# Cross attention on one core: keys split ahead, two copies side by side, scores in two half-width passes

## The chip, the cores and the metric

The kernel runs on one core of a Trainium2 chip. The metric is the device time of one execution in microseconds, as the median of several runs. Before the change it is 922.41 us (three runs, 921.37 to 923.53).

## The reference, cut to what matters

A two-layer transformer block on 16 rows of 128 tokens with 256 features. Layer 0 is a convolution-like mixer with a feed-forward part (8 shared units, 8 routed experts). Layer 1 is causal attention of the normed activations (queries) over a context (keys and values are both `ctx_2048`), with 16 heads of 16 features, then a routed feed-forward part (34 units). The change touches the attention of layer 1 only:

```
x = x + tanh(g) * attention(layernorm(x), ctx, ctx)        # per layer; here layer 1
scores = einsum('bhqd,bhkd->bhqk', q, k) * HEAD_DIM**-0.5   # 16 heads of 16 features
scores = where(causal, -inf, scores)
out    = einsum('bhqk,bhkd->bhqd', softmax(scores), v)
```

All products have to be close to float32. TensorE is used with operands rounded to a shorter form (fp32r); a float32 number is split in a high part (rounded) and a low part (the rest), and products of parts are added.

## The kernel before, in words

The kernel has four stages, which follow one another on every engine: the mixer (`ctx`), the feed-forward part of layer 0 (`f0`, 64 steps K), the attention (`att`) and the feed-forward part of layer 1 (`f1`, 136 steps). Every engine has its own program, written out by hand, with semaphores between them.

The attention works on 64 quads n: block b = n // 4 is one row of 128 tokens, t = n % 4 picks four heads. One quad goes through these steps:

- `scores` (TensorE, L1458 to L1463): a bf16 pass of 512 columns puts the causal mask in a bank, then two fp32r passes of 512 columns add the products. The weights are `q_split_t` (128 rows: for each of the four heads 16 features of the high part and 16 of the low part, 64 high rows and 64 low rows); the moving tiles are `k_blocks_hi` and `k_blocks_lo`, in which each head's keys stand in their own 128 columns and the rest is zero.
- `maxima` and `shifted` (VectorE, L1642, L1648): the row maximum over each head's 128 columns, and the scores less the maximum, written to `y`.
- `turned` (TensorE, L1470): four f32 transposes into another bank.
- `probs` (ScalarE, L1611): exp of that bank to `activated`.
- `values` (TensorE, L1481): four products with `v_slot`, which stand as eight instructions in the trace.

The program of TensorE (`c_tensor`, L1558) takes, in iteration n, `turned(n)`, `scores(n + 2)`, `values(n)`, and behind them whatever else falls due. At t = 2 that is `out_rows` (L1490: four transposes that bring the result of the block before to rows), at t = 3 `query_turned(b + 2)` (L1374: four transposes of the split queries of block b + 2). Then comes `turned(n + 1)`.

The program of ScalarE (`c_scalar`, L1606) takes in iteration n: at t = 0 `out_copy` (L1504, the result's bank to SBUF), then `probs(n)`, then at t = 0 `query_copy` (L1382, the turned queries to SBUF), then `key_hi(n + 4)` (L1343, which rounds the loaded keys to the high part), at t = 2 `query_normed` (L1354), at t = 3 `query_hi` (L1361). GpSimd makes the low parts (`key_lo`, L1347; `query_lo`, L1366) and two small layer norm steps (L140, L153). SyncE issues the loads of keys (256 KB a quad, six slots, L1332) and of values (L1337).

At the end of `f0` some of this is done ahead: in the last 16 of its 64 steps SyncE loads the first six key tiles, ScalarE splits the first four, TensorE turns the queries of blocks 0 and 1 (L1374, eight and five steps before the end), and in step 63 TensorE makes the scores of quads 0 and 1 before its last product.

In `f0` a step is 12 fp32r passes of 512 columns (L666), ScalarE's silu (L446), VectorE's product (L541, L546), the split of `y` in ScalarE and VectorE (L465, L311), and 6 passes of 512 columns (L702). TensorE has one step's L666 ahead of each L702.

Of the kernel before, what the change touches and what calls it, by code (L numbers as in the profile page):

```python
# [61 lines left out]
def build(nc, x, ctx_win, k_blk, v_rows, g_x, g_f, kpad, d_skip, wu0, rw0, eb0, wu1, rw1, br1,  # L62
          ident_c, anti_c, identb_c, causal_c, out):
    top = ExitStack()
    with top:
# [24 lines left out]
        gates1 = nc.dram_tensor("gates1", (E1, T), F32, kind="Internal").ap()  # L90
        x_mid = nc.dram_tensor("x_mid", (T, D), F32, kind="Internal").ap()
# [76 lines left out]
        def feed_forward(tag, E, U, gated, wu, gates, tgcol, route, final):  # L168
# [219 lines left out]
            def sync(sp):  # L388
# [16 lines left out]
                for K in range(NK):  # L405
                    Nu = K // 2
                    if K % 2 == 0 and Nu + S < 2 * U:
                        weights(sp, Nu + S)
                    for m in range(NBLK):
                        if GATES_STORE[m] == K:  # L410
                            store_gates(m)
                    if gated and K == 0:
                        for q in range(NB - 2, NB):
                            ctx.store_mixed(q)
                    if gated and K == 2:
                        for g in range(NB // BPB):
                            ctx.load_in_order(g)
                    gate_rows(K)
                    if not final and K == NK - 16:
                        attention_loads(sp)  # L420
# [7 lines left out]
            def gpsimd(pool):  # L428
                if not gated:
                    for Nu in range(2, 4):  # L430
                        w_lo(pool, Nu)
                    for K in range(FIRST):
                        y_lo(pool, K)
                deviations(pool, tag, 1)
                if not final:
                    deviations(pool, "c", 0)
                    shifts(pool, "c", 0)
                    attention_ahead_pool(pool)

            def scalar(act):  # L440
# [49 lines left out]
                for K in range(NK):  # L490
# [34 lines left out]
                    if not final:  # L525
                        attention_ahead_act(act, NK - K)
# [774 lines left out]
        KLR, KR, SR, DR, PR = 6, 4, 3, 3, 3  # L1301
# [3 lines left out]
        KM = sb("k_blocks_sb", [P, KLR, 4 * P])  # L1305
        K1 = sb("k_blocks_hi", [P, KR, 4 * P], F32R)
        K2 = sb("k_blocks_lo", [P, KR, 4 * P], F32R)
        V = sb("v_slot", [P, 2, NH1, 32])
        xc = sb("xn_c", [P, 2, D])
        xs = sb("xn_split", [P, 2, 4, 2, 64], F32R)  # L1310
        Q1 = sb("q_split_t", [P, 2, 4, P], F32R)
        mem.out_scaled = sb("out_scaled", [P, 2, 2, BLK])
        s_sh = shift_sems["c"][1]
        s_kl = ctx.s_cq + ctx.s_cg[0:2]
        s_vl = [ctx.s_cg[2], ctx.s_kt[0]]
        LOADED = 16
        s_cc = sem("c_causal_loaded")
        s_k1 = sem("c_k_hi_ready")
        s_k2 = sem("c_k_lo_ready")
        s_n = sem("c_normed")  # L1320
# [17 lines left out]

        def key_hi(act, n):
            act.wait_ge(s_kl[n % KLR], LOADED + 16 * (n // KLR + 1))  # L1340
            if n >= KR:
                act.wait_ge(s_s, n - KR + 1)
            act.activation(K1[:, n % KR, :], KM[:, n % KLR, :], ACT.Copy).then_inc(s_k1, 1)  # L1343

        def key_lo(pool, n):
            pool.wait_ge(s_k1, n + 1)
            pool.tensor_tensor(K2[:, n % KR, :], KM[:, n % KLR, :], K1[:, n % KR, :].bitcast(F32),  # L1347
                               ALU.subtract).then_inc(s_k2, 1)
# [7 lines left out]

        def query_hi(act, b):
            act.wait_ge(s_n, b + 1)
            if b >= 2:
                act.wait_ge(s_xt, b - 1)  # L1360
            act.activation(xs[:, b % 2, :, 0, :], xc[:, b % 2, :].rearrange("p (q f) -> p q f", q=4),  # L1361
                           ACT.Copy).then_inc(s_hi, 1)

        def query_lo(pool, b):
            pool.wait_ge(s_hi, b + 1)
            pool.tensor_tensor(xs[:, b % 2, :, 1, :], xc[:, b % 2, :].rearrange("p (q f) -> p q f", q=4),  # L1366
                               xs[:, b % 2, :, 0, :].bitcast(F32), ALU.subtract).then_inc(s_lo, 1)

        def query_turned(pe, b):
            pe.wait_ge(s_lo, b + 1)  # L1370
            if b > 0:
                pe.wait_ge(s_qt, b)
# [5 lines left out]
        def query_copy(act, b):  # L1378
            act.wait_ge(s_xt, b + 1)
            if b >= 2:  # L1380
                act.wait_ge(s_s, 4 * (b - 1))
            act.activation(Q1[:, b % 2].rearrange("p t q -> p (t q)"), x_bank, ACT.Copy, scale=SCALE1).then_inc(s_qt, 1)  # L1382

        def attention_loads(sp):
            for n in range(KLR):
                load_keys(sp, n)
            sp.dma_start(causal[:], causal_c).then_inc(s_cc, 16)
            sp.dma_start(identb[:], identb_c).then_inc(s_cc, 16)
            load_values(sp, 0)
            load_values(sp, 1)  # L1390

        def attention_ahead_act(act, left):

            if left in (12, 11, 4):
                query_normed(act, {12: 0, 11: 1, 4: 2}[left])
            if left in (11, 10, 3):
                query_hi(act, {11: 0, 10: 1, 3: 2}[left])
            if left in (9, 8, 7, 6):
                key_hi(act, 9 - left)
            if left in (6, 3):  # L1400
                query_copy(act, {6: 0, 3: 1}[left])

        def attention_ahead_pe(pe, left):

            if left in (8, 5):
                query_turned(pe, {8: 0, 5: 1}[left])

        def attention_ahead_pool(pool):
            query_lo(pool, 0)
            query_lo(pool, 1)  # L1410
            for n in range(KR):
                key_lo(pool, n)
# [8 lines left out]
        def attention():  # L1421
# [30 lines left out]
            def scores(pe, n):  # L1452
# [6 lines left out]
                pe.wait_ge(s_k2, n + 1)  # L1459
                if t == 0:  # L1460
                    pe.wait_ge(s_qt, b + 1)
                pe.matmul(s_bank(n), Q1[:, b % 2, t, :], K1[:, n % KR, :], start=False, stop=False)  # L1462
                pe.matmul(s_bank(n), Q1[:, b % 2, t, :], K2[:, n % KR, :], start=False, stop=True).then_inc(s_s, 1)  # L1463
# [70 lines left out]
            def c_sync(sp):  # L1534
                for n in range(KLR, NQ):
# [6 lines left out]
            def c_gpsimd(pool):  # L1542
                for n in range(NQ):
                    b, t = n // 4, n % 4
                    if n + KR < NQ:
                        key_lo(pool, n + KR)
# [11 lines left out]
            def c_tensor(pe):  # L1558
# [3 lines left out]
                for n in range(NQ):  # L1562
# [15 lines left out]
                    if t == 3 and b + 2 < NB:  # L1578
                        query_turned(pe, b + 2)
# [11 lines left out]
                    if n in (49, 57):  # L1591
                        pe.wait_ge(s_qt, b + 2)
# [5 lines left out]
                    if n == 54:  # L1598
                        pe.wait_ge(s_qt, b + 2)
# [6 lines left out]
            def c_scalar(act):  # L1606
# [6 lines left out]
                for n in range(NQ):  # L1613
                    b, t = n // 4, n % 4
                    if t == 0 and b > 0:
                        out_copy(act, b - 1)
                    probs(n)
                    if t == 0 and b > 0 and b + 1 < NB:
                        query_copy(act, b + 1)
# [12 lines left out]
                    if n + KR < NQ:  # L1632
                        key_hi(act, n + KR)
# [151 lines left out]
```

## Time and profile before

| | us |
|---|---|
| median of three runs | 922.41 |
| the profiled execution's own time | 921.7 |
| its span | 919.9 |
| TensorE busy | 888.2 (97%) |
| VectorE busy | 604.5 (66%) |
| ScalarE busy | 550.3 (60%) |
| GpSimd busy | 191.7 (21%) |
| granted TensorE clock, mean | 0.992 |

The stages in the span: mixer to about 105 us, `f0` to 386.7, attention to about 520, `f1` to the end. A busy TensorE is not TensorE at its peak, since a matmul's record holds its way through the array too; so the order of starts and ends in the timeline says more than the busy share.

### The profile page before, as it was taken

How to read it: one execution, taken by the hardware profiler on the slowest of the kernel's cores; microseconds unless marked ns; L12 is line 12 of the kernel's file. 1: busy time of each engine (PE TensorE's matmuls, PEld its weight loads, DVE VectorE, ACT ScalarE, POOL GpSimd, SP SyncE). 2: the span in 40 equal slices, each digit the busy share in tenths (PEclk: the TensorE clock that was granted, in tenths of full speed). 3: DMA queues.
4: the chain of work that ended last, by engine and by line, in shares of the span. 5: the costliest groups of instructions: out<-in, count | busy, mean ns of one | idle time of the engine just before them, and what ended most of it. 6: DMA issues, size and time to landing. Idle time of an engine off the chain costs nothing.

```text
span 919.9 us, 13780 instructions
## 1 busy us (share of the span) xinstructions
PE 888.2 (97%) x4704; PEld 711.0 (77%) x4704; DVE 604.5 (66%) x1238; ACT 550.3 (60%) x955; POOL 191.7 (21%) x163
## 2 busy tenths in 40 slices
PE   6799999999999999989999989999999999999997
PEld 5699887787888888756666667878788888888886
DVE  6699764465645656598898776657765465665554
ACT  3225353434543344468888766777777877777774
POOL 5799200000000102067776420000000000000000
PEclk8899999999999999999999999999999999999999
DMA  8203150442211532135553334434444344444443
GB/s 299 76 14 121 41 149 18 132 121 81 74 53 50 182 104 64 40 115 172 173 165 126 113 96 140 124 121 141 133 150 143 102 134 144 145 138 147 150 127 103
DMA packets 62564, 108.54 MB, mean 118 GB/s; under 512 B 7808, under 2 KB 18432, under 8 KB 62112
## 3 DMA queue, kind: packets, MB, share of 16 engines
q1 hardware_dynamic: 61776, 107.53, 37.0%
q8 instruction: 38, 0.62, 0.3%
q14 instruction: 30, 0.25, 0.1%
q10 hardware_dynamic: 720, 0.14, 0.1%
HBM read 103.13 MB, written 4.52 MB: 117 GB/s over the span
## 4 chain that ended last, share of the span: by engine, by line
PE 84%; DVE 6%; ACT 3%; POOL 2%; DMA 2%; issue 2%; SPq 0%; DVEq 0%; ACTq 0%; POOLq 0%
PE bank L666 37%; PE bank L702 29%; PE bank L1470 2%; PE bank L1481 2%; PE bank L1153 1%; PE bank L1152 1%; PE bank L1150 1%; PE bank L1166 1%; PE bank L365 1%; PE bank L1463 1%; DMA k_blocks_sb<-in_k_blk 1%; PE bank L1462 1%; PE bank L1458 1%; DMA x_mixed<-in_x 1%; PE bank L346 1%
## 5 line engine op out<-in xcount | busy, mean ns | idle before, releaser
L465 ACT ACTIVATE y_hi<-y 128x512 fp32r<-128x512 f32 x200 | 124.1, 621 | 81.3 <-DVE y L546 80.7
L560 DVE TENSOR_TENSOR y<-y,gate_rows 128x512 f32<-128x512 f32 x124 | 85.8, 692 | 120.4 <-ACT y L454 118.2
L702 PE MATMUL bank<-y_hi,w_hi 128*128 128x512 f32 x400 | 157.3, 393 | 1.5 <-DVE y_lo L311 1.0
L702 PE MATMUL bank<-y_lo,w_hi 128*128 128x512 f32 x400 | 156.7, 392 | 0.0
L702 PE MATMUL bank<-y_hi,w_lo 128*128 128x512 f32 x400 | 156.1, 390 | 0.0
L311 DVE TENSOR_TENSOR y_lo<-y,y_hi 128x512 fp32r<-128x512 f32 x196 | 134.4, 686 | 29.9 <-ACT y_hi L465 29.6
L448 ACT ACTIVATE activated<-bank 128x512 f32<-128x512 f32 x136 | 81.1, 597 | 80.8 <-PE bank L666 76.2
L666 PE MATMUL bank<-x_hi_first,w_hi 128*128 128x512 f32 x264 | 106.3, 403 | 0.7 <-DVE w_lo L306 0.7
L666 PE MATMUL bank<-x_hi_first,w_lo 128*128 128x512 f32 x264 | 104.3, 395 | 0.0
L666 PE MATMUL bank<-x_lo_first,w_hi 128*128 128x512 f32 x264 | 104.2, 395 | 0.0
L666 PE MATMUL bank<-x_hi_last,w_hi 128*128 128x512 f32 x264 | 104.0, 394 | 0.0
L666 PE MATMUL bank<-x_hi_last,w_lo 128*128 128x512 f32 x264 | 103.0, 390 | 0.0
L666 PE MATMUL bank<-x_lo_last,w_hi 128*128 128x512 f32 x264 | 102.8, 390 | 0.0
L1347 POOL TENSOR_TENSOR k_blocks_lo<-k_blocks_sb,k_blocks_hi 128x512 fp32r<-128x512 f32 x64 | 81.9, 1282 | 59.7 <-ACT k_blocks_hi L1343 59.6
L702 PEld LDWEIGHTS bank<-y_hi,w_hi 128*128 128x128 f32 x400 | 75.1, 188 | 20.2 <-DVE y_lo L311 2.8
L454 ACT ACTIVATE y<-activated 128x512 f32<-128x512 f32 x136 | 86.0, 632 | 4.3
L702 PEld LDWEIGHTS bank<-y_hi,w_lo 128*128 128x128 f32 x400 | 75.2, 188 | 16.2
L702 PEld LDWEIGHTS bank<-y_lo,w_hi 128*128 128x128 f32 x400 | 75.2, 188 | 16.2
L446 ACT ACTIVATE activated<-bank 128x512 f32<-128x512 f32 x64 | 38.3, 598 | 77.5 <-PE bank L666 77.5
L306 DVE TENSOR_TENSOR w_lo<-w_raw,w_hi 128x512 fp32r<-128x512 f32 (+1 forms) x96 | 75.1, 783 | 10.9 <-ACT w_hi L302 4.9
L302 ACT ACTIVATE w_hi<-w_raw 128x512 fp32r<-128x512 f32 (+1 forms) x100 | 69.8, 698 | 12.6 <-PE bank L702 12.6
L666 PEld LDWEIGHTS bank<-x_hi_first,w_hi 128*128 128x128 f32 x264 | 49.6, 188 | 12.4 <-DVE w_lo L306 1.0
(155 smaller groups left out, 1436.5 us busy)
## 6 DMA issues: line engine op xcount, KB each, us to landing
gate_rows<-gates SPq DMA_DIRECT2D x156, 256.0 KB, 3.7
w_raw<-in_wu SPq DMA_DIRECT2D x68, 256.0 KB, 2.6
k_blocks_sb<-in_k_blk SPq DMA_DIRECT2D x64, 256.0 KB, 4.6
w_raw<-in_wu SPq DMA_DIRECT2D x32, 384.0 KB, 3.2
v_slot<-in_v_rows SPq DMA_DIRECT2D x16, 256.0 KB, 2.6
ctx_windows<-in_ctx_win SPq DMA_DIRECT2D x3, 1024.0 KB, 10.8
toeplitz<-in_kpad SPq DMA_DIRECT2D x4, 512.0 KB, 9.1
x_mixed<-in_x SPq DMA_DIRECT2D x4, 512.0 KB, 9.2
```

What stands on the lines that cost most here:

```text
L302: act.activation(mem.whi[:, Nu % S, 0:WC], mem.wraw[:, Nu % S, 0:WC], ACT.Copy).then_inc(s_wh, 1)
L306: eng.tensor_tensor(mem.wlo[:, Nu % S, 0:WC], mem.wraw[:, Nu % S, 0:WC], mem.whi[:, Nu % S, 0:WC].bitcast(F32), ALU.subtract).then_inc(s_w ...
L311: eng.tensor_tensor(mem.ylo[:, K % S, :], mem.y[:, K % S, :], mem.yhi[:, K % S, :].bitcast(F32), ALU.subtract).then_inc(s_yl, 1)
L446: act.activation(mem.r[:, K % S, :], bk(2 * K % 3), ACT.Silu).then_inc(s_ac, 1)
L448: act.activation(mem.r[:, K % S, :], bk(K % 3), ACT.Relu).then_inc(s_ac, 1)
L454: act.activation(mem.y[:, K % S, :], mem.r[:, K % S, :], ACT.Square).then_inc(s_sq, 1)
L465: act.activation(mem.yhi[:, K % S, :], mem.y[:, K % S, :], ACT.Copy).then_inc(s_yh, 1)
L560: dve.tensor_tensor(mem.y[:, K % S, :], mem.y[:, K % S, :], gate, ALU.mult).then_inc(s_yd, 1)
L666: last = pe.matmul(o, w_[:, Nu % S, wc], x_[p][:, c, xs], start=(m == 0), stop=(m == 5))
L702: last = pe.matmul(acc(s)[:, c, :], w_[:, Nu % S, wc], y_[:, K % S, :], start=(n == 0 and m == 0), stop=(n == U - 1 and m == 2), skip_grou ...
L1347: pool.tensor_tensor(K2[:, n % KR, :], KM[:, n % KLR, :], K1[:, n % KR, :].bitcast(F32), ALU.subtract).then_inc(s_k2, 1)
L1470: last = pe.transpose(turn_bank(n)[:, g * P:(g + 1) * P], Ds[:, n % DR, g, :], ident[:])
```

## The change

The keys are no longer loaded as zero-padded blocks and split quad by quad in the attention. Instead:

1. While `f0` runs (steps 16 to 42), the context comes in compact form (`k_rows`, two blocks of 128 x 256 a load, 8 loads), ScalarE rounds it to the high part (8 instructions of 128 x 512), GpSimd makes the low part (8 of 128 x 512), and SyncE stores both parts to a new DRAM array `k_parts` (four stores of 128 KB each time, 32 in all).
2. GpSimd zeroes the eight slots of the one key tile (`K1`, 128 x 4096) once.
3. In the attention each quad's keys are loaded by two DMAs that write only the non-zero places; each row of `k_parts` is written to two neighbouring partitions. `key_hi` and `key_lo` are gone.
4. The 128 rows of a pass now hold two heads: 64 rows a head, for each feature its four part products (key high and low by query high and low). A pass has 256 columns and two heads; two passes, with different weights, make a quad's scores. The mask pass stays.
5. So the queries' tile doubles: `query_hi` and `query_lo` write 128 x 512 instead of 128 x 256, with stride-2 places and each element twice, and a block's queries are turned in two groups (`query_turned(b, 0)`, `query_turned(b, 1)`) of four transposes, with one copy each. The second group stands at t = 0, behind `values(4b)`; the two copies stand ahead of `probs` at t = 0 and t = 1. The transposes are fp32r and not f32, with a rounded identity made once.

```diff
-        KLR, KR, SR, DR, PR = 6, 4, 3, 3, 3
+        KR, SR, DR, PR = 8, 3, 3, 3
...
+        def split_hi(act, i):
+            act.wait_ge(s_kr[i % 2], 16 * (i // 2 + 1))
+            if i >= 2:
+                act.wait_ge(s_ks[i % 2], 64 * (i // 2))
+            raw, high, _ = split_places(i)
+            act.activation(high, raw, ACT.Copy).then_inc(s_k1, 1)
+
+        def split_lo(pool, i):
+            pool.wait_ge(s_k1, i + 1)
+            raw, high, low = split_places(i)
+            pool.tensor_tensor(low, raw, high.bitcast(F32), ALU.subtract).then_inc(s_k2, 1)
+
+        def store_parts(sp, i):
+            sp.wait_ge(s_k1, i + 1)
+            sp.wait_ge(s_k2, i + 1)
+            for part, rows in enumerate(split_places(i)[1:]):
+                for j in range(2):
+                    place = k_parts[2 * i + j].rearrange("(g s d) f -> g s d f", s=2, d=HD1)[:, part]
+                    sp.dma_start(place, rows[:, j * D:(j + 1) * D].bitcast(F32)).then_inc(s_ks[i % 2], 16)
+
+        def blocks_zeroed(pool):
+            pool.memset(K1[:].rearrange("p n f -> p (n f)").bitcast(F32), 0.0).then_inc(s_kz, 1)
...
         def load_keys(sp, n):
-            if n >= KLR:
-                sp.wait_ge(s_k2, n - KLR + 1)
-            sp.dma_start(KM[:, n % KLR, :], k_blk[n]).then_inc(s_kl[n % KLR], 16)
+            if n >= KR:
+                sp.wait_ge(s_s, n - KR + 1)
+            for hh in range(2):
+                first = k_parts.offset + (2 * P * (n // 4) + 64 * (n % 4) + 32 * hh) * D
+                place = bass.AP(k_parts.tensor, first, [[D, 2 * HD1], [0, 2], [1, D]])
+                sp.dma_start(K1[64 * hh:64 * hh + 64, n % KR, hh * D:hh * D + D].bitcast(F32), place).then_inc(s_kl[n % KR], 16)
...
         def query_hi(act, b):
...
-            act.activation(xs[:, b % 2, :, 0, :], xc[:, b % 2, :].rearrange("p (q f) -> p q f", q=4),
-                           ACT.Copy).then_inc(s_hi, 1)
+            act.activation(part_rows(b, 0), copies_of(xc[:, b % 2, :]), ACT.Copy).then_inc(s_hi, 1)
...
             for t in range(4):
-                last = pe.transpose(x_bank[:, t * P:(t + 1) * P],
-                                    xs[:, b % 2, t].rearrange("p s f -> p (s f)").bitcast(F32), ident[:])
+                last = pe.transpose(x_bank[:, t * P:(t + 1) * P].bitcast(F32R), xs[:, b % 2, t, a, :], ident_r[:])
...
-            if left in (9, 8, 7, 6):
-                key_hi(act, 9 - left)
-            if left in (6, 3):
-                query_copy(act, {6: 0, 3: 1}[left])
+            if left in (10, 7, 4, 1):
+                query_copy(act, (10 - left) // 6, (10 - left) // 3 % 2)
...
-            if left in (8, 5):
-                query_turned(pe, {8: 0, 5: 1}[left])
+            if left in (12, 9, 6, 3):
+                query_turned(pe, (12 - left) // 6, (12 - left) // 3 % 2)
...
-                pe.matmul(s_bank(n), Q1[:, b % 2, t, :], K1[:, n % KR, :], start=False, stop=False)
-                pe.matmul(s_bank(n), Q1[:, b % 2, t, :], K2[:, n % KR, :], start=False, stop=True).then_inc(s_s, 1)
+                blocks = K1[:, n % KR, :].rearrange("p (h a k) -> p h a k", h=2, a=2)
+                for a in range(2):
+                    last = pe.matmul(s_bank(n)[:, a * 2 * P:(a + 1) * 2 * P], Q1[:, b % 2, a, t, :], blocks[:, :, a, :],
+                                     start=False, stop=(a == 1))
+                last.then_inc(s_s, 1)
...
                     if t == 3 and b + 2 < NB:
-                        query_turned(pe, b + 2)
+                        query_turned(pe, b + 2, 0)
+                    if t == 0 and b > 0 and b + 1 < NB:
+                        query_turned(pe, b + 1, 1)
...
                         out_copy(act, b - 1)
+                    if t < 2 and b > 0 and b + 1 < NB:
+                        query_copy(act, b + 1, t)
                     probs(n)
-                    if t == 0 and b > 0 and b + 1 < NB:
-                        query_copy(act, b + 1)
...
-                    if n + KR < NQ:
-                        key_hi(act, n + KR)
```

## Rows read from the trace of the kernel before

**Rows 1.** Windows: stretch, its length, busy us of PE, PEld, DVE, ACT, POOL, clock, DMA.
```profile
240.00:380.00 140.00, 140.00 (x634) 115.52 (x633) 79.80 (x154) 61.31 (x101) 10.62 (x9) 1.00 0.26 84
402.30:520.00 117.70, 114.94 (x1009) 74.15 (x1010) 101.77 (x190) 95.28 (x182) 85.93 (x74) 1.00 0.49 160
```

**Rows 2.** Timeline of one plain quad: start us, us, engine, line, instruction.
```profile
426.85 0.43 PE L1481 MATMUL bank<-activated,v_slot 128*32 128x128 f32 x8
427.21 0.66 PE L1470 MATMUL bank<-ident,y 128*128 128x128 f32 x4
427.90 0.60 ACT L1611 ACTIVATE activated<-bank 128x512 f32<-128x512 f32 x1 [0.53 <-PE bank L1470]
427.92 0.19 PEld L1463 LDWEIGHTS bank<-k_blocks_lo,q_split_t 128*128 128x128 f32 x1
428.15 0.39 PE L1463 MATMUL bank<-k_blocks_lo,q_split_t 128*128 128x512 f32 x1
428.55 0.16 PEld L1481 LDWEIGHTS bank<-activated,v_slot 128*32 128x32 f32 x8 [0.44 <-ACT activated L1611]
```

**Rows 3.** Waits from 402.3 to 520 us: who, for whom, us in total, times, longest.
```profile
PEld bank L1481 <- ACT activated L1611: 27.0, 58, 0.9
...
DVE max L1642 <- PE bank L1463: 8.1, 24, 0.9
...
ACT xn_f L339 <- POOL neg_mean_scaled L153: 1.1, 1, 1.1
```

**Rows 4.** Timeline of a quad with query transposes, TensorE's rows.
```profile
430.69 0.43 PE L1481 MATMUL bank<-activated,v_slot 128*32 128x128 f32 x8
431.04 0.66 PE L1374 MATMUL bank<-ident,xn_split 128*128 128x128 f32 x4
431.54 0.60 PE L1470 MATMUL bank<-ident,y 128*128 128x128 f32 x4
...
432.82 0.42 PE L1481 MATMUL bank<-activated,v_slot 128*32 128x128 f32 x8
```

**Rows 5.** The same quad, ScalarE's rows.
```profile
430.53 0.62 ACT L1343 ACTIVATE k_blocks_hi<-k_blocks_sb 128x512 fp32r<-128x512 f32 x1
431.05 0.41 ACT L1361 ACTIVATE xn_split<-xn_c 128x256 fp32r<-128x256 f32 x1
431.36 0.59 ACT L1504 ACTIVATE o_t<-bank 128x512 f32<-128x512 f32 x1
432.17 0.60 ACT L1611 ACTIVATE activated<-bank 128x512 f32<-128x512 f32 x1 [0.23 <-PE bank L1470]
432.67 0.59 ACT L1382 ACTIVATE q_split_t<-bank 128x512 fp32r<-128x512 f32 x1
```

**Rows 6.** Timeline: four f32 transposes with 8-column weights, and four with 8 moving columns.
```profile
145.95 0.60 PE L711 MATMUL bank<-ident,gtf 128*8 128x128 f32 x4
...
101.05 0.41 PE L378 MATMUL bank<-ident,logits_t 8*128 8x8 f32 x4
```

**Rows 7.** The chain of waits in f0: start us, us, what.
```profile
287.69 2.72 PE bank L666 x12
```

**Rows 8.** The chain of waits from 390 to 402 us, shares by line.
```profile
by line: DVE y L1648 28.9%; DVE max L1642 25.1%; DVE stats L248 16.4%; DVE X L244 15.2%; issue 11.1%; DVE mv L130 4.7%; DVE neg_mean L146 1.3%; DVE vpe L133 0.3%
```

**Rows 9.** The chain of waits from 470 to 480 us.
```profile
472.42 1.28 POOL k_blocks_lo L1347
473.70 1.61 POOL rstd L140
```

**Rows 10.** Timeline of an f0 step: the split of y, and the product that needs it.
```profile
287.90 0.68 DVE L311 TENSOR_TENSOR y_lo<-y,y_hi 128x512 fp32r<-128x512 f32 x1
...
290.25 0.39 PE L702 MATMUL bank<-y_hi,w_hi 128*128 128x512 f32 x1
```

**Rows 11.** Timeline of f0's end, ScalarE.
```profile
385.48 2.54 ACT L472 ACTIVATE out_scaled<-bank,tg 128x512 f32<-128x512 f32 x4
```

**Rows 12.** DMA issues from 402.3 to 520 us: KB each, median us to landing.
```profile
k_blocks_sb<-in_k_blk SPq DMA_DIRECT2D x51, 256.0 KB, 4.3
```

More of the change, by code:

```diff
@@ L418, in sync @@
                     gate_rows(K)
-                    if not final and K == NK - 16:
-                        attention_loads(sp)
+                    if not final:
+                        if K in (16, 18):
+                            load_raw(sp, (K - 16) // 2)
+                        if 21 <= K < 45 and K % 3 == 0:
+                            i = (K - 21) // 3
+                            store_parts(sp, i)
+                            if i + 2 < NB // 2:
+                                load_raw(sp, i + 2)
+                        if K == NK - 16:
+                            attention_loads(sp)
+                        if NK - 16 <= K < NK - 16 + KR:
+                            load_keys(sp, K - NK + 16)
                 if final:
@@ L435, in gpsimd @@
                 if not final:
+                    for i in range(NB // 2):
+                        split_lo(pool, i)
+                    blocks_zeroed(pool)
                     deviations(pool, "c", 0)
@@ L525, in scalar @@
                     if not final:
+                        if 19 <= K < 43 and K % 3 == 1:
+                            split_hi(act, (K - 19) // 3)
                         attention_ahead_act(act, NK - K)
@@ L1337, in load_values @@
             sp.dma_start(V[:, b % 2].rearrange("p h d -> p (h d)"), v_rows[b]).then_inc(s_vl[b % 2], 16)
[L1339 to L1348, printed above, removed]
         def query_normed(act, b):
@@ L1355, in query_normed, with copies_of, part_rows @@
                            scale=rstd[:, b:b + 1]).then_inc(s_n, 1)
+        def copies_of(view):
+            return view.rearrange("p (g f) -> p g f", f=HD1).unsqueeze(2).broadcast_to((P, NH1, 2, HD1))
+        def part_rows(b, part):
+            return xs[:, b % 2].rearrange("p t a (h d f s) -> p (t a h) d f s", h=2, d=2, s=2)[:, :, :, :, part]
         def query_hi(act, b):
@@ L1410, in attention_ahead_pool @@
             query_lo(pool, 1)
-            for n in range(KR):
-                key_lo(pool, n)
             query_lo(pool, 2)
@@ L1534, in c_sync @@
             def c_sync(sp):
-                for n in range(KLR, NQ):
+                for n in range(KR, NQ):
                     load_keys(sp, n)
@@ L1598, in c_tensor @@
                     if n == 54:
-                        pe.wait_ge(s_qt, b + 2)
+                        pe.wait_ge(s_qt, 2 * b + 4)
                         f1.logits(pe, 0, x_bank)
@@ L1740 @@
     heads = c.reshape(NB, P, 4, 4, HD1).transpose(0, 2, 3, 4, 1)
-    blocks = np.zeros((NB, 4, 2, 4, HD1, 4, P), np.float32)
-    for h in range(4):
-        blocks[:, :, :, h, :, h, :] = heads[:, :, None, h]
-    blocks = blocks.reshape(NB * 4, P, 4 * P)
+    keys = heads.reshape(NB, 4, 2, 2, HD1, P).transpose(0, 1, 3, 4, 2, 5).reshape(NB, P, D)
     values = np.zeros((NB, P, NH1, 32), np.float32)
@@ L1765 @@
     arrays = {
-        "x": mixed, "ctx_win": windows, "k_blk": blocks, "v_rows": values,
+        "x": mixed, "ctx_win": windows, "k_rows": keys, "v_rows": values,
         "g_x": a["g_xattn"], "g_f": a["g_ffn"], "kpad": kpad, "d_skip": a["L0_xattn_D"],
```

75 lines of the change are left out of this document (46 added, 29 removed).

## The prediction

> **What bounds the kernel now.** I read the windows first, then the timeline of single quads, then the waits, because a busy share says little here. TensorE is busy all of the 140 us of f0 and 114.9 of the 117.7 us of the attention from 402.3 us on [rows 1]. In f0 that is a true bound: products follow each other without a gap [rows 7]. In the attention it is not. The reader should follow one plain quad [rows 2]: `values` begins at 426.85, `turned` is behind it at 427.21 (0.36 later) and its last result is there at 427.87; exp begins at 427.90 and ends at 428.50; the next `values` begins at 428.55. The period is 0.36 + 0.66 + 0.03 + 0.60 + 0.05 = 1.70 us, and it is one chain: values, turned, exp, values. The scores lie beside it. Their last pass begins at 428.15, and a 512-column fp32r pass holds TensorE for 2.72 / 12 = 0.227 us [rows 7], so TensorE was free at 428.38 and stood 0.17 us until exp had ended. The table of waits says the same for the whole stage: the weight load of `values` waited for exp 58 times in 58 quads [rows 3].
>
> What does lengthen the chain is all that TensorE does between `values` and the next `turned`. At t = 3 the four query transposes stand there: `values` at 430.69, L1374 at 431.04, `turned` only at 431.54 with its end at 432.14, exp at 432.17, the next `values` at 432.82 [rows 4, 5]. That quad takes 2.13, so the group costs 0.43, or 0.108 a transpose. With `out_rows` at t = 2 a block takes 4 x 1.70 + 2 x 0.43 = 7.67 us. The first quads, to 402 us, go by another chain, of VectorE: maximum, shift, residual, moments [rows 8]. VectorE is no bound later: it waited for scores 24 times [rows 3].
>
> **The change, part by part.** The sum is made against the profiled execution, 921.7 us (span 919.9 and 1.8 around it); the median of the runs is 0.7 above it.
>
> *Scores in two half-width passes.* Before: two passes of 0.227. After: at best 256 / 512 of that each, 0.114. But each needs a weight load of its own, whose record is 0.19 long [rows 2]; at worst a pass is as long as now. So TensorE gains between 0 and 0.23 a quad. On the chain this is worth 0: TensorE waits for exp already, with 0.17 to spare. The maximum begins 0.1 to 0.2 earlier, and VectorE has nothing late waiting for it. If a short pass were dearer than a long one, the 0.17 would cover 0.08 a pass; I take no loss.
>
> The Trainium skill, "TensorE: Matmul & The Clock Gate", section "Back-to-back issue gap", gives 262 cycles of 2.4 GHz for 256 columns, 0.109 us a pass (an estimate from that page), which would make the full gain on TensorE. The rows above say that this time isn't on the path; the rule alone would predict a faster kernel.
>
> *Second group of query transposes.* A block now has eight, and the second four stand at t = 0 behind `values(4b)`, in front of `turned(4b + 1)`, on the chain, for b = 1 to 14. They are fp32r and were f32. No row of before has an fp32r transpose, so bounds: 0.108 each as in f32 [rows 4] above. Below: four f32 transposes with 8-column weights take 0.60, the same as with 128 [rows 4, 6], so the moving side sets their rate; with 8 moving columns four take 0.41 [rows 6]. The difference, 0.19 over three spacings, is 0.063 at most, so an fp32r transpose that streams a column a cycle could come down to 0.05 to 0.06. I keep both ends: A, 0.06 each, four for 0.25; B, 0.108 each, four for 0.43. Above B stands the fp32r pass rate, 0.227 each, four for 0.9, if a short fp32r instruction gains nothing.
>
> The Trainium skill, same page, section "LDWEIGHTS", says that a weight load takes its columns over 1.2 GHz, 0.107 us for 128. By that rule it would be B. The 0.41 for four loads of 128 columns [rows 6] speaks against it for f32 transposes; for fp32r no run here shows it.
>
> *ScalarE's order.* The copies of the turned queries now stand ahead of exp at t = 0 and t = 1. Copy after copy begins about 0.50 later (432.17 to 432.67), a 512-column rounding takes 0.52 (430.53 to 431.05) [rows 5]. At t = 0, from the start of exp(4b - 1): exp 0.50, the doubled `query_hi` 0.52 to 1.02; `out_copy` can begin when `values` is done, 0.65 + 0.43 + 0.04 = 1.12; `query_copy` then at 1.62, exp at 2.12 (A). For B the copy waits for its transposes, 0.65 + 0.36 + 0.66 + 0.04 = 1.71, and exp begins at 2.21. Before it was 2.13. At t = 1: transposes done at 1.01 + 0.66 - 3 x 0.05 = 1.52 and seen 0.04 later (A), or at 1.71 (B), then the copy, exp at 2.06 or 2.21 in place of 1.70. A block so grows by 2.12 + 2.06 - 3.83 = 0.35 (A) or 2.21 + 2.21 - 3.83 = 0.59 (B). Block 1's lies under the VectorE chain at the start, so 13 blocks: +4.6 (A), +7.7 (B).
>
> *Key splits out of the attention.* This takes 0.52 x 4 from ScalarE and 1.28 x 4 from GpSimd a block. Neither is on the chain in a plain block. It was in one place: the layer norm step of GpSimd (L140) stood behind a `key_lo` until 473.70, and ScalarE's L339, in front of exp(43), waited 1.1 for it [rows 3, 9]. GpSimd is now idle at that time, so I take the 1.1 back; at the least 0, if normed rows and the longer `query_hi` crowd ScalarE there instead.
>
> *Splitting ahead in f0.* ScalarE has 61 us and VectorE 80 of 140 busy [rows 1], GpSimd almost nothing, and TensorE is the bound. 8 x 0.52 on ScalarE, 8 x 1.28 on GpSimd, the memset (by 1.28 for 512 columns at most 10 us) lie beside it. `y_lo` ends at 288.58 and is needed at 290.25, 1.67 to spare [rows 10], more than one GpSimd instruction could hold VectorE. SyncE now waits in steps 21, 24, ... 42 for the splits; behind it are gate rows and weights. By its slots it may run four steps ahead; the store in its step 3i + 21 waits for ScalarE's step 3i + 19, so the fetches behind it come about two steps, 2 x 4.08 = 8 us, before their use (a step is 18 passes of 0.227). A landing of some 4.3 behind four stores [rows 12] fits. Zero, with up to +3 if one fetch comes late.
>
> *Turns ahead in f0.* Four groups in place of two on a TensorE that is the bound: 4 x 0.25 - 2 x 0.43 = +0.14 (A), +0.87 (B). In step 63 the last copy, 0.50, now stands ahead of `out_scaled`, which runs back to back until TensorE can go on [rows 11]; half of that had room, about +0.2.
>
> *Loads.* Two DMAs of 64 KB in place of one of 256 KB with a landing of 4.3 [rows 12]. A key tile is asked for 8 quads ahead; after a load of values, which waits for an older block, still 4 quads, over 7 us. Hidden.
>
> *Sum.* A: 4.6 + 0.1 + 0.2 - 1.1 = +3.8. B: 7.7 + 0.9 + 0.2 - 1.1 = +7.7. I can't tell A from B by a row; the operation is nearest to the f32 transpose and the data type to a pass of one column a cycle. I take +4.7, between them and nearer to A: 926.4 against 921.7, or 927.1 against the median; rounded 927.0. Own range 925.0 to 931.0.
>
> **Rivals.**
> 1. *TensorE paces the quads after all.* Then 58 quads gain 0.23 from the halved passes, -13.2, the second turns of 0.25 to 0.43 cost +3.3 to +5.6, f0 +0.3 to +1.1, the stall -1.1 comes back: 912 to 915 against the median. It decides if `values` begins when the scores' last pass is through, and not when exp ends. For it: 97.7% busy [rows 1]. Against: 58 waits in 58 [rows 3]. In milder form (half of it) 918. 10%.
> 2. *The extra turn is nearly free.* A holds, the copies hide in ScalarE's new idle time, and the stall comes back: 13 x (2 x 0.25 - 0.43) + 0.3 - 1.1 = +0.1, about 922.5. For it: ScalarE loses 2.1 us of work a block. Against: the copy stands in front of exp by program order. 13%.
> 3. *Short fp32r instructions are dear.* A transpose of 0.227: the group 0.9, a block +0.5 from the first and +0.9 from the second turn and 0.1 of ScalarE, 13 x 1.5 = 19.5, f0 4 x 0.9 - 0.9 = +2.7: about 943. 6%.
> 4. *f0 loses its feeding.* A gate row or weight late behind SyncE's waits, or VectorE held by GpSimd beyond its 1.67: 8 times up to 1 us on top of the forecast: 930 to 935. 8%.
>
> **How the numbers follow.** The forecast has 63%, the rivals 10, 13, 6 and 8. No change is what a measurement can't tell, 0.2% or 1.8 us, 920.6 to 924.3. Faster: rival 1 and a little of rival 2, 0.11. Same: the rest of rival 2 and the low edge of the forecast, 0.16. Slower: 0.73. The range 922.0 to 931.5 leaves rival 1, part of 4, and rival 3 outside.
>
> **What would show it.** Right: `values` still begins 0.05 after exp; plain quads (t = 2) stay at 1.70; quads 4b to 4b + 1 go from 1.70 to 2.05 or 2.20, with L1374's successor between `values` and `turned`; TensorE waits more, not less, before `values`. The four fp32r transposes tell A from B by their length, 0.45 or 0.60. f0 keeps its period of 4.08 us. Wrong: a plain quad under 1.70 (rival 1), a second turn with no later exp (rival 2), gaps of TensorE in f0 (rival 4).

## The result: 0.4% slower, and the profile after

The changed kernel takes 925.9 us in the median (7 runs, 925.12 to 927.15), the kernel before 922.01 in the runs beside it (7 runs). The ratio is 1.0043, with a 95% interval of 1.0031 to 1.0054. The profiled execution takes 925.9 us (span 924.1) against 921.7 (span 919.9): +4.2 us, and this is what the rows below have to explain. Forecast were 926.4 for that execution and 927.0 for the median.

The page of the kernel after, busy time of each engine and the two new kinds of DMA (count, size, median us to landing):

```profile
PE 877.6 (95%) x4747; PEld 714.1 (77%) x4768; DVE 602.3 (65%) x1238; ACT 532.4 (58%) x916; POOL 132.9 (14%) x108
...
k_blocks<-k_parts SPq DMA_DIRECT2D x128, 64.0 KB, 2.4
k_parts<-xn_split SPq DMA_DIRECT2D x32, 128.0 KB
```

Every engine has less to do: TensorE 10.6 us, ScalarE 17.9, GpSimd 58.8. The time is longer all the same. The windows of the same two stages, columns as in [rows 1]:

```profile
240.00:380.00 140.00, 139.83 (x633) 114.53 (x632) 80.49 (x154) 62.60 (x103) 15.95 (x11) 1.00 0.33 103
404.00:520.00 116.00, 100.71 (x1009) 75.01 (x1026) 95.52 (x186) 72.94 (x136) 17.92 (x16) 1.00 0.34 101
```

TensorE now stands idle for 15 of 116 us in the attention, where it did for 2.8 of 117.7. Its waits say for whom; the first row answers to the first of [rows 3]:

```profile
PEld bank L1536 <- ACT activated L1666: 26.7, 56, 0.9
...
PE bank L1536 <- ACT activated L1666: 15.3, 56, 0.7
```

Before, the weight load of `values` came early to exp nearly every time, but its products hardly stood idle:

```profile
PE bank L1481 <- ACT activated L1611: 1.1, 3, 0.7
```

Now the products have a gap of their own (15.3 us). The chain is values, turned, exp, values, as before. A stretch with both query groups of a block shows how it got longer, TensorE first (L1428 turns queries, L1525 is `turned`, L1516 the scores, L1536 `values`):

```profile
432.95 0.43 PE L1536 MATMUL bank<-activated,v_slot 128*32 128x128 f32 x8 [0.24 <-ACT activated L1666]
433.31 0.55 PE L1428 MATMUL bank<-ident_r,xn_split 128*128 128x128 f32 x4
433.69 0.62 PE L1525 MATMUL bank<-ident,y 128*128 128x128 f32 x4
434.18 0.58 PE L1516 MATMUL bank<-k_blocks,q_split_t 128*128 128x256 f32 x2
435.07 0.43 PE L1536 MATMUL bank<-activated,v_slot 128*32 128x128 f32 x8 [0.31 <-ACT activated L1666]
435.43 0.54 PE L1428 MATMUL bank<-ident_r,xn_split 128*128 128x128 f32 x4
435.80 0.62 PE L1525 MATMUL bank<-ident,y 128*128 128x128 f32 x4
436.27 0.38 PE L1510 MATMUL bank<-causal,identb 128*128 128x512 bf16 x1
436.29 0.58 PE L1516 MATMUL bank<-k_blocks,q_split_t 128*128 128x256 f32 x2
```

And ScalarE in the same stretch, which answers to [rows 5]:

```profile
432.30 0.60 ACT L1666 ACTIVATE activated<-bank 128x512 f32<-128x512 f32 x1 [1.05 <-PE bank L1525]
432.79 0.68 ACT L1414 ACTIVATE xn_split<-xn_c 128x512 fp32r<-128x512 f32 x1
433.44 0.60 ACT L1559 ACTIVATE o_t<-bank 128x512 f32<-128x512 f32 x1
433.94 0.59 ACT L1435 ACTIVATE q_split_t<-bank 128x512 fp32r<-128x512 f32 x1
434.41 0.60 ACT L1666 ACTIVATE activated<-bank 128x512 f32<-128x512 f32 x1
436.00 0.60 ACT L1435 ACTIVATE q_split_t<-bank 128x512 fp32r<-128x512 f32 x1 [0.99 <-PE bank L1428]
436.50 0.59 ACT L1666 ACTIVATE activated<-bank 128x512 f32<-128x512 f32 x1
```

From exp to exp: 434.41 - 432.30 = 2.11 at t = 0 (before 2.13) and 436.50 - 434.41 = 2.09 at t = 1 (before 1.71; 2.08 and 1.70 in most blocks). A group takes 433.69 - 433.31 = 0.38 in front of `turned`. At t = 1 two things end almost together. `turned` is through at 435.80 + 0.62 = 436.42, so exp could begin at 436.45. The copy in front of it begins at 436.00 and lets exp begin 0.50 later, at 436.50: the copy decides, but only by 0.05. `values` still begins 0.05 after exp's end.

The starts of the 64 exps and of the 64 first products L718 of `f0`, set against those of before, give the whole ledger, in us (steps 28 to 33 and so on are steps of `f0`; exp(n) is the exp of quad n):

| stretch | after less before |
|---|---|
| mixer | +0.06 |
| f0, steps 28 to 33 | +0.77 |
| f0, four groups of turns in place of two | +0.65 |
| from step 62 of f0 to exp(0) | +0.35 |
| attention, 13 quads with t = 1 (9 x 0.38, 3 x 0.35, 1 x 0.11) | +4.57 |
| attention, quads with t = 0 (44 and 48: +0.43, the others -0.20) | +0.23 |
| attention, exp(43) | -1.06 |
| attention, quad 5 | -0.47 |
| attention, the rest (quad 61 -0.25; 14, 15, 31 -0.23; others -0.08) | -0.56 |
| f1 | -0.33 |
| sum | +4.2 |

### The profile page after: what moved, and what is told of

It reads as the page before. It is cut to its first block, busy times and chain, and to the rows that moved or that the text cites. A ratio compares the mean times of both kernels' runs of the same rounds, so it can differ in the third digit from the quotient of the medians.

```text
span 924.1 us, 13885 instructions
## 1 busy us (share of the span) xinstructions
PE 877.6 (95%) x4747; PEld 714.1 (77%) x4768; DVE 602.3 (65%) x1238; ACT 532.4 (58%) x916; POOL 132.9 (14%) x108
## 4 chain that ended last, share of the span: by engine, by line
PE 81%; ACT 6%; DVE 5%; issue 3%; POOL 2%; DMA 1%; SPq 0%; DVEq 0%; ACTq 0%; POOLq 0%
PE bank L682 37%; PE bank L718 29%; ACT activated L1666 3%; PE bank L1536 2%; PE bank L1525 2%; PE bank L1169 1%; PE bank L1168 1%; PE bank L366 1%; PE bank L1166 1%; PE bank L1182 1%; PE bank L1428 1%; PE bank L1545 1%; DMA x_mixed<-in_x 1%; PE bank L347 1%; ACT xn_split L1414 1%
## 5 line engine op out<-in xcount | busy, mean ns | idle before, releaser
L576 DVE TENSOR_TENSOR y<-y,gate_rows 128x512 f32<-128x512 f32 x124 | 85.8, 692 | 119.6 <-ACT y L468 117.6
L718 PE MATMUL bank<-y_hi,w_hi 128*128 128x512 f32 x400 | 157.4, 393 | 1.3 <-DVE y_lo L312 0.8
L718 PE MATMUL bank<-y_lo,w_hi 128*128 128x512 f32 x400 | 156.6, 391 | 0.0
L718 PE MATMUL bank<-y_hi,w_lo 128*128 128x512 f32 x400 | 156.0, 390 | 0.0
L462 ACT ACTIVATE activated<-bank 128x512 f32<-128x512 f32 x136 | 81.3, 597 | 80.1 <-PE bank L682 75.6
L718 PEld LDWEIGHTS bank<-y_hi,w_hi 128*128 128x128 f32 x400 | 75.0, 188 | 21.2 <-DVE y_lo L312 3.7
L718 PEld LDWEIGHTS bank<-y_hi,w_lo 128*128 128x128 f32 x400 | 75.1, 188 | 16.4
L718 PEld LDWEIGHTS bank<-y_lo,w_hi 128*128 128x128 f32 x400 | 75.1, 188 | 16.1
L460 ACT ACTIVATE activated<-bank 128x512 f32<-128x512 f32 x64 | 38.3, 598 | 74.3 <-PE bank L682 74.1
L1666 ACT ACTIVATE activated<-bank 128x512 f32<-128x512 f32 x64 | 38.3, 598 | 41.4 <-PE bank L1525 41.3
```

Of the source, the lines that this page charges most:

```text
L460: act.activation(mem.r[:, K % S, :], bk(2 * K % 3), ACT.Silu).then_inc(s_ac, 1)
L462: act.activation(mem.r[:, K % S, :], bk(K % 3), ACT.Relu).then_inc(s_ac, 1)
L576: dve.tensor_tensor(mem.y[:, K % S, :], mem.y[:, K % S, :], gate, ALU.mult).then_inc(s_yd, 1)
L718: last = pe.matmul(acc(s)[:, c, :], w_[:, Nu % S, wc], y_[:, K % S, :], start=(n == 0 and m == 0), stop=(n == U - 1 and m == 2), skip_grou ...
L1666: act.activation(PT[:, n % PR, :], turn_bank(n), ACT.Exp).then_inc(s_e, 1)
```

## Experiments

Theory: exp's chain sets the length of a quad, the second query group and its copy lengthen it, and everything that left TensorE was beside the chain. Rival: TensorE sets the pace, and with it the narrow passes. The first four kernels are the changed kernel with one edit each. "Ratio" is the ratio to the kernel before, in runs beside it. `...` in an edit or a profile stands for lines left out.

**One score pass left out**, so that half of each quad's scores isn't computed.

```diff
-                for a in range(2):
+                for a in range(1, 2):
                     last = pe.matmul(s_bank(n)[:, a * 2 * P:(a + 1) * 2 * P], ...
```

> The kernel after the change, with the first of the two score passes of each quad left out (the scores of two heads of four are then the mask alone). Theory (the chain values, turned, exp, values sets the pace and the scores lie beside it): plain quads stay at 1.70 us, the quads behind a second turn at 2.08, the time stays within 1 us of 925.9; TensorE's wait before values grows by 0.12 us. Rival (TensorE paces the quads): 0.12 us less in each of some 58 quads, about 919.

Measured: 926.13 us, ratio to before 1.0046 (1.0031 to 1.0060). The quads keep 1.69 and 2.08.

**Each score pass twice.**

```diff
-                for a in range(2):
+                for i in range(4):
+                    a = i % 2
...
```

> The kernel after the change, with each of the two score passes done twice (scores are then twice as large where a key is). This adds 2 x 0.116 = 0.23 us of TensorE a quad, as much as the change took away. Theory: TensorE waits 0.24 to 0.31 us for exp in each quad, so all of it is hidden, and the time stays within 1 us of 925.9. Rival (TensorE paces the quads): +0.23 x 58 = +13, about 939.

Measured: 926.24 us, ratio 1.0046 (1.0031 to 1.0061), intervals 1.70 and 2.08. From one pass to four, 0.35 us of TensorE in every quad, the time doesn't move. Rival 1 is out: in this order the narrow passes are worth nothing.

**f32 transposes of the queries**, which is case B made real.

```diff
-  pe.transpose(x_bank[...].bitcast(F32R), xs[:, b % 2, t, a, :], ident_r[:])
+  pe.transpose(x_bank[...], xs[:, b % 2, t, a, :].bitcast(F32), ident[:])
```

> The kernel after the change, with the query transposes in f32 as before instead of fp32r. Theory: a group of four costs 0.43 us on the chain in place of 0.35, and the copy in front of exp comes 0.10 later: quads 4b to 4b + 2 grow by 0.1 each, two a block in some 11 blocks, and 4 x 0.08 in f0: +2 to +3, about 928.5 (my case B). Rival (the type of the transposes is of no matter, ScalarE's order sets these quads): no difference, 925.9.

Measured: 928.61 us, ratio 1.0072 (1.0055 to 1.0088). TensorE's rows of the same two quads:

```profile
433.98 0.43 PE L1536 MATMUL bank<-activated,v_slot 128*32 128x128 f32 x8 [0.24 <-ACT activated L1666]
434.34 0.66 PE L1428 MATMUL bank<-ident,xn_split 128*128 128x128 f32 x4
434.83 0.60 PE L1525 MATMUL bank<-ident,y 128*128 128x128 f32 x4
...
436.17 0.43 PE L1536 MATMUL bank<-activated,v_slot 128*32 128x128 f32 x8 [0.29 <-ACT activated L1666]
```

A group is 0.49 here (434.34 to 434.83) and 0.38 with fp32r. From exp to exp it is 2.20 at t = 0 and 2.18 at t = 1, where the changed kernel has 2.11 and 2.08. The 0.11 of TensorE comes back as 0.09 and 0.10 of time.

**No second group and copy in the attention** for blocks 2 to 15 (their scores use old weights in the second pass).

```diff
+            if a == 1 and b >= 2:
+                pe.sem_inc(s_xt, 1)
+                return
```

and the same in `query_copy`.

> The kernel after the change without the second group of query transposes and without its copy for the blocks 2 to 15 (their second score pass works on the tile of block 0 or 1). Theory: the quad at t = 1 falls from 2.08 to 1.70 in 13 blocks, -4.9: about 921.0, a little below the kernel before, since the exp stall at quad 43 and a VectorE stall near 400 us are gone. Rival (the loss of the change is in f0 or in the loads): the time stays near 925.9.

Measured: 921.26 us, ratio 0.9995 (0.9986 to 1.0005). The quads with t = 1 are back at 1.70. So the second group and its copy together cost 4.6 us, and the rest of the change, losses and gains added up, is worth nothing that can be measured. The two were taken out together, and at t = 1 they end within 0.05 of each other, so no run shows what either costs alone.

**The order of TensorE.** If the chain is what counts, the groups belong not between `values` and `turned` but between scores and `values`, where TensorE waits for exp. Two kernels move them there for quads 8 to 43: the kernel before (`out_rows` and `query_turned`), and the changed kernel (all three groups; the second one now at t = 1, the copies behind exp).

```diff
+                    early = 8 <= n < 44
+                    if early and t == 1:
+                        query_turned(pe, b + 1, 1)
+                    if early and t == 2:
+                        out_rows(pe, b - 1)
+                    if early and t == 3:
+                        query_turned(pe, b + 2, 0)
                     if n < NQ - 1:
                         values(pe, n)
...
```

> The kernel before the change, with out_rows and the query transposes of the quads 8 to 43 placed between the scores and values (in TensorE's wait for exp) instead of behind values. Theory (chain): TensorE has 0.17 us free there and a group takes 0.43, so each group still costs 0.26 in place of 0.43: 18 groups x 0.17 = 3.1 less, about 919. Rival (the groups cost the same wherever they stand, since TensorE is the bound): 922.

> The kernel after the change, with all three groups of a block (out_rows, both query groups) in the quads 8 to 43 placed between the scores and values, the second query group at t = 1, and the copies of the turned queries behind exp instead of in front. Theory: here the narrow passes are worth something, since TensorE has 0.24 to 0.31 us free: a query group of 0.35 costs about 0.08, out_rows 0.15, a block takes about 7.1 instead of 8.05 us, 9 blocks: -8, about 918, a little below the same step on the kernel before. VectorE (about 6.8 us a block) becomes the next bound. Rival (narrow passes are worth nothing anywhere): no better than the same step made on the kernel before plus the cost of one more group, about 922.

Measured: 921.14 us (ratio 0.9994, 0.9985 to 1.0004) for the kernel before in that order, which is a miss of the forecast 919, and 916.94 us (0.9951, 0.9939 to 0.9963) for the changed one. One of its ten executions, the profiled one, took 921.68 and the others 916.27 to 917.82. That one had a granted clock of 0.50 from 392 us on for a while and lost 3.4 us against before in `f1`, between its steps 5 and 7. TensorE in the kernel before so reordered, a quad with `out_rows` (L1490):

```profile
427.68 0.58 PE L1462 MATMUL bank<-k_blocks_hi,q_split_t 128*128 128x512 f32 x1
428.10 0.39 PE L1463 MATMUL bank<-k_blocks_lo,q_split_t 128*128 128x512 f32 x1
428.33 0.60 PE L1490 MATMUL bank<-ident,o_t 128*128 128x128 f32 x4
428.86 0.43 PE L1481 MATMUL bank<-activated,v_slot 128*32 128x128 f32 x8
```

Its exp ends at 427.85 + 0.60 = 428.45, so `values` comes 0.41 later and not 0.05: of a group of 0.43 only 0.08 is hidden. The wide scores have filled the gap up to 0.17 before `values` (0.12 before exp's end), and in this place the group takes 0.53 until `values` begins (428.33 to 428.86). The 18 quads behind a group gain up to 0.08 each, and the stall of before at exp(43) only moves: exp(41) comes 1.27 later after its predecessor and exp(43) 1.14 earlier. From exp(0) to exp(63) 0.9 us are left of it.

**Splits and turns of f0 at other steps.** The changed kernel with the eight splits at steps 19, 22, 25, 34, 36, 38, 40, 42 and the turns and copies at the end one step earlier.

```diff
-                        if 19 <= K < 43 and K % 3 == 1:
-                            split_hi(act, (K - 19) // 3)
+                        if K in SPLITS:
+                            split_hi(act, SPLITS.index(K))
...
-            if left in (10, 7, 4, 1):
+            if left in (11, 8, 5, 2):
...
```

> The kernel after the change, with two moves in f0 alone: the splits of the context in steps 19, 22, 25, 34, 36, 38, 40 and 42 instead of every third from 19 (so none stands in steps 28 and 31, where ScalarE reloads its table for silu and VectorE makes the routing weights), and the query turns and copies ahead one step earlier (so no copy stands between the last y_hi and the table load for exp). Theory: the 0.77 us that f0 lost between steps 28 and 33 come back, and some 0.6 of the end: about 924.6. Rival (these come from the loads or stores, not from the two engines' order): 925.9.

Measured: 924.67 us, ratio 1.0030 (1.0017 to 1.0042). The drift of steps 28 to 33 is gone (the products keep their distance from those of before within 0.02 from step 0 to step 51), and from step 62 to exp(0) it is 0.49 shorter than in the changed kernel. All splits from step 28 on were moved together, so this run doesn't tell step 28 from step 31; the rows further down do.

**Both**, the new order of the attention and the new steps of f0:

> The kernel after the change with the moves of both e6 and e7. Theory: they add, about 916.5, faster than both kernels. Rival: the quads of the attention are then paced by VectorE and the moves in f0 are partly lost: 918.

Measured: **915.46 us** (914.49 to 916.08, 4 runs), ratio 0.9928 (0.9913 to 0.9943), the best of all. TensorE in two quads of it, the first with `out_rows` (L1546), the second with a query group (L1429):

```profile
418.42 0.59 PE L1517 MATMUL bank<-k_blocks,q_split_t 128*128 128x256 f32 x2
418.85 0.60 PE L1546 MATMUL bank<-ident,o_t 128*128 128x128 f32 x4
419.38 0.42 PE L1537 MATMUL bank<-activated,v_slot 128*32 128x128 f32 x8
419.73 0.66 PE L1526 MATMUL bank<-ident,y 128*128 128x128 f32 x4
420.23 0.38 PE L1511 MATMUL bank<-causal,identb 128*128 128x512 bf16 x1
420.26 0.59 PE L1517 MATMUL bank<-k_blocks,q_split_t 128*128 128x256 f32 x2
420.68 0.46 PE L1429 MATMUL bank<-ident_r,xn_split 128*128 128x128 f32 x4
421.08 0.42 PE L1537 MATMUL bank<-activated,v_slot 128*32 128x128 f32 x8
```

Exps begin at 418.59, 420.43, 422.13 and 423.83. One block takes 1.70 + 1.70 + 1.70 + 1.83 = 6.93 us (before 7.67, after 8.02). The f32 group starts 428.33 - 427.68 = 0.65 after the scores in the kernel before and 418.85 - 418.42 = 0.43 here. That difference, 0.22, is what the narrow passes give, and it takes the excess behind exp's end from 0.36 to 0.13. The fp32r group is shorter by 0.13 again (420.68 to 421.08, 0.40) and hidden whole.

**The same with each score pass twice**, which puts 0.23 us a quad back on TensorE. Nothing else differs from the kernel with both edits, so the difference between the two is what narrow passes are worth in this order:

> The kernel of e8 with each of the two score passes of 256 columns issued twice, so that TensorE has 0.23 us more of scores in every quad (4 x 0.116 in place of 2 x 0.116). If the narrow passes earn their time only in the order of e8, where the groups of transposes stand between scores and values: quads with the softmax rows' transposes (one in four, 9 blocks) get 0.13 to 0.23 longer from exp's end to the values, and quads with a query's group, which have 0.05 there, grow by 0 to 0.2 each; 9 x (0.15 to 0.6) = +1.5 to +5, so 917 to 920.5. If ScalarE and VectorE pace the quads in this order too, with TensorE beside them: 915.5, as e8.

Measured: 921.55 us, ratio 0.9999 (0.9990 to 1.0009), 6.1 us slower than without. In TensorE's rows the groups start that much later:

```profile
421.98 0.83 PE L1518 MATMUL bank<-k_blocks,q_split_t 128*128 128x256 f32 x4
422.64 0.46 PE L1429 MATMUL bank<-ident_r,xn_split 128*128 128x128 f32 x4
423.03 0.43 PE L1538 MATMUL bank<-activated,v_slot 128*32 128x128 f32 x8
```

422.64 - 421.98 = 0.66 in place of 0.42. Three of four quads take 0.23 to 0.24 more, 26 in all, and the kernel 6.0 us more from exp(0) to exp(63). The same 0.23 a quad that was worth 0 in the order of the change is worth all of itself where a group stands behind the scores. It went over the forecast of up to +5: the quads with a query group lost 0.23 too, where I had given them some slack.

**Without GpSimd's low part** (the high part is stored twice, so the scores lack the keys' low parts):

```diff
-            pool.tensor_tensor(low, raw, high.bitcast(F32), ALU.subtract).then_inc(s_k2, 1)
+            pool.sem_inc(s_k2, 1)
```

> The changed kernel, in which the low part of every key split is left out on GpSimd (the high part is stored in its place, so the scores lack the low part of the keys). If VectorE at step 31 of f0 is held up by GpSimd's subtraction (1.33 us for an instruction that takes 0.22 elsewhere, a row 0.4 late), then that instruction takes about 0.22 here and the steps 28 to 33 of f0 lose 0.3 to 0.5 us of their 0.77; the time 925.4. If it is waiting for memory traffic or for its own operands, it stays at 1.3 and the drift stays at 0.77; 925.9.

Measured: 926.71 us (4 runs), ratio 1.0057 (1.0039 to 1.0075): no faster than the changed kernel, where 925.4 was expected. VectorE and GpSimd in the changed kernel:

```profile
252.14 1.30 POOL L1368 TENSOR_TENSOR xn_split<-v_slot,xn_split 128x512 fp32r<-128x512 f32 x1 [11.56 <-ACT xn_split L1363]
252.19 1.33 DVE L850 TENSOR_TENSOR wt<-rd,pd 128x64 f32<-128x64 f32 x1
```

and VectorE in the kernel without the subtraction:

```profile
251.93 0.22 DVE L850 TENSOR_TENSOR wt<-rd,pd 128x64 f32<-128x64 f32 x1
```

So GpSimd does hold VectorE here, for 1.1 us. But little follows from it for TensorE. The drift of the products against before, by step:

| | steps 28 to 31 | 31 to 32 | 32 to 33 |
|---|---|---|---|
| after | +0.26 | +0.36 | +0.15 |
| after, with each pass twice | +0.26 | 0.00 | +0.09 |
| after, without second groups | +0.27 | 0.00 | +0.08 |
| without the low part | +0.26 | 0.00 | 0.00 |

Three more kernels with the same splits (one pass, f32 turns, all groups moved) have +0.39 to +0.46 in the first column, 0.00 in the second and +0.10 or +0.11 in the third. The first column is the split at step 28, which stays without the low part; why it is larger in those three wasn't looked for. The hold-up costs 0.1, not the 0.3 to 0.5 that I expected. The 0.36 stands only in the one execution of after, and has its own cause there, a gate row that landed late (`[0.44 <-DMA gate_rows<-gates]` in front of VectorE's L557 at 249.46). Where the kernel without the low part loses this again in its profiled execution can be read: at the start of the attention TensorE ran at 1.2 GHz for a while (below), and in `f1`, between its steps 5 and 6, it loses 0.86 against before where after gains 0.30 (VectorE's L576 begins at 555.17 there and at 554.27 in after). Whether its other runs have the same isn't known.

## Why the prediction was right, point by point

- *Chain, and halved passes worth 0 on it*: right. Plain quads stay at 1.70 with one, two or four passes. On TensorE the gain is nearly the full one, 0.116 a pass (434.642 to 434.758 between the ends of two) against 0.227. The forecast counted 0.17 us from the scores to exp's end; by its own rows that is the time to `values`, and 0.12 to exp's end. Nothing hung on it there.
- *Second turn, t = 1*: forecast 2.06 (A) or 2.21 (B) for 1.70; measured 2.08. The mechanism of both cases was right, the copy in front of exp. The transposes lie between the two: of the four of a group the last three start at 433.425, 433.511 and 433.600, so 0.087 apart. A had 0.06, B 0.108 (which f32 transposes do take). The sign that was to tell A from B, a length of 0.45 or 0.60 (the sum itself used 0.51 and 0.66), came out at 0.54. That the interval was so near to A is in part luck: two of the three distances between starts were 0.03 longer than A had them, but the first was as A had it (0.119, where f32 has 0.166) and a single record was 0.02 shorter than in f32 (0.25 and 0.27). So the last transpose ends 0.54 after the group's start, where A had 0.51. At t = 0 forecast 2.12, measured 2.11, with ScalarE's instructions in the order and at the distances forecast. The Trainium skill, "TensorE: Matmul & The Clock Gate", section "LDWEIGHTS (loading the stationary operand)", gives the load of 128 columns 0.107 us, and by that rule case B was to be expected. The 0.087 measured is shorter, so such a load doesn't set the pace of fp32r transposes here.
- *13 blocks*: forecast +4.6 (A), measured +4.57 at t = 1 and +0.23 at t = 0. Leaving out the group and its copy gives 4.6 back.
- *exp(43)*: forecast -1.1, measured -1.06 (3.20 to 2.14).
- *Turns ahead in f0*: forecast +0.1 to +0.9, measured +0.65 (four groups of 0.38 to 0.42 for two of 0.48 or 0.49). In TensorE's own time A's 0.25 was too small.
- *Copy before `out_scaled`*: mis-sized, +0.2 forecast, +0.49 measured (+0.35 from step 62 to exp(0), since `out_scaled` itself was 0.13 shorter). ScalarE at the end of f0, which answers to [rows 11]:

```profile
384.90 0.63 ACT L479 ACTIVATE y_hi<-y 128x512 fp32r<-128x512 f32 x1 [1.56 <-DVE y L562]
385.44 0.58 ACT L1435 ACTIVATE q_split_t<-bank 128x512 fp32r<-128x512 f32 x1
386.04 1.28 ACT L1502 ACT_TABLE_LOAD   x1
387.33 0.20 ACT L1502 ACTIVATE exp_table<-tg 128x1 f32<-128x1 f32 x1
387.44 2.41 ACT L486 ACTIVATE out_scaled<-bank,tg 128x512 f32<-128x512 f32 x4
```

  I had given half of the copy room. But it stands in front of the load of exp's table (1.28) as well, and from `y_hi` on this is a chain without a gap to the transposes of L234, which begin at 389.90. None of the copy had room. One step earlier it costs nothing: in the kernel with both moves `out_scaled` begins 2.05 after `y_hi` as before (385.43 after 383.38), where after has 2.54.
- *Splitting ahead in f0*: 0 forecast, +0.77 measured in the profiled execution and 0.35 to 0.56 in the five others that have the same steps. "ScalarE has 61 us ... of 140 busy" was the step that failed: what counts is where its instruction stands. At step 28 the split stood in front of a table load that silu waits for:

```profile
238.44 0.26 ACT L493 ACTIVATE sc<-lgf 128x64 f32<-128x64 f32 x1
238.60 0.62 ACT L1363 ACTIVATE xn_split<-v_slot 128x512 fp32r<-128x512 f32 x1
239.23 1.28 ACT L460 ACT_TABLE_LOAD   x1
```

  Before, the table load follows at 238.66. GpSimd's subtraction at step 31 held VectorE as rival 4 has it, but all of that except 0.1 was within VectorE's slack. The Trainium skill, "SBUF — State Buffer", section "Who interferes with whom", says that a VectorE instruction with two SBUF inputs contends with a GpSimd one that reads SBUF, for ports that only one of them can hold. The trace agrees: L850 ends at 253.52, 0.08 after GpSimd's subtraction, and takes 0.22 without it.
- *Not foreseen, in favour*: in quad 5 VectorE's L133 took 0.65 beside a GpSimd instruction before, and the same instruction takes 0.17 after (-0.47). Small stalls of before are gone (-0.48 with quad 61); their causes weren't looked for.
- *Loads*: hidden, as forecast. Their landing is 2.4 in place of 4.3.

So the total was close partly by luck, because errors met: f0 and its end cost 1.77 where 0.3 to 1.1 was forecast, and the attention gained 1.0 in small places. The +4.7 was itself no case worked out but a choice between A (+3.8) and B (+7.7); measured is +4.2. Rival 1 fell with the first two experiments, rival 2 with the 0.38 at t = 1, rival 3 with 0.087 a transpose, and of rival 4 no more than 0.1 from GpSimd and one late gate row (0.36) in one execution came true.

## What to carry to other kernels

Before work is taken off an engine, see whether the chain passes through it; if it doesn't, the freed time is worth nothing until something of the chain is moved into it. Here 0.23 a quad was worth 0 us in the order given, and 6.1 us once the transposes stood in the wait for exp. Before an instruction is slipped into a half-idle engine, look at what follows it in program order: if a table load that another engine waits for stands there, the instruction delays that by its whole length, as the copy did here (0.49 us). In the best kernel the next limit is near: VectorE is busy for 60.6 of the 65 us from 405 to 470.

## What the runs showed of the hardware

- In the changed kernel's attention an fp32r transpose of 128 x 128 starts 0.087 us after the last, an f32 one 0.108 or 0.109; four in front of `turned` take 0.38 and 0.49. The pace depends on what stands ahead: behind the narrow scores of the best kernel the four fp32r transposes start at 420.680, 420.744, 420.806 and 420.891. A 256-column fp32r pass takes 0.116, though the record of its weight load is 0.19 long.
- TensorE's clock fell in some executions and not in others with the same wait ahead of it. Six profiled executions have a wait of 1.91 to 1.95 us before L234; four of them (f32 turns, no second group, all groups moved, no low part) show a granted clock of 0.50 to 0.57 in a stretch of 2 us within the next 4, and two (after, one pass) don't. The six with 1.36 to 1.69 don't either. One execution of each kernel makes no rule, but the late copy does lengthen this wait: it is 1.36 before, and 1.36 to 1.47 in the three kernels that have the copy one step earlier. At the end of f0 TensorE waited 1.95 us for `out_scaled` in after and went on at 2.4 GHz; without the low part it waited 1.91 and went on at 1.2 GHz (granted clock 0.50). The window 390 to 392 of that kernel:

```profile
390.00:392.00 2.00, 2.00 (x12) 1.94 (x10) 1.60 (x4) 0.00 (x0) 0.00 (x0) 0.50 0.00 0
```

  Its eight transposes L234 took 1.67 in place of 1.09 and exp(0) came 1.0 late: at 392.08, where 391.10 would be due (after's 391.47, less the 0.37 by which this kernel was ahead at step 62). Of that 0.83 came back in quads 1 and 2, where VectorE sets the pace.
- The mixer ends up to 0.85 us earlier or 0.67 later than before in single executions, and VectorE waited 0.44 for a gate row in one. A difference under 1 us between two single profiles of this kernel has to be found in its rows, not in its total.
